# Weights of the shared and the first expert requested piece by piece along the token loop of a fused cross-attention and mixture-of-experts kernel

## Chip, cores and metric

One core of one Trainium2 chip. The metric is the device time of one execution in microseconds (us); lower is better.

## What is computed

The input is `x` (8 batches of 256 tokens, 256 wide, float32, so 16 tiles of 128 tokens) with a context of 77 keys per batch. Two residual layers follow each other, each behind a layer norm:

```python
x = x + tanh(g_xattn) * attention(layernorm(x), ctx, ctx, mask, Wq, Wk, Wv, Wo, ...)   # 16 heads of 16
x = x + tanh(g_ffn)   * ffn(layernorm(x), ...)
# ffn of a token row t:
#   combine = the top 2 of softmax(t @ gate_w.T) over 8 experts, renormalised
#   out  = sum over e of combine[e] * (gelu(t @ W1[e] + b1[e]) @ W2[e] + b2[e])   # 256 -> 1024 -> 256
#   out += gelu(t @ sW1 + sb1) @ sW2 + sb2                                        # the shared expert
```

## The kernel before

The five engines run programs of their own, written out by hand in the source, with counting semaphores between them. Nothing is reordered: the order of the code is the order on each engine and on each engine's DMA queue.

**Setup (to about 52 us).** The context is transposed and keys and values are projected. The keys make a round trip through memory (`move_keys`, lines 299 to 306: `moved_k` out, three pieces of `kstack` back in). The queries of a token tile make such a trip too: `move_queries(t)` (308 to 319) on SyncE (SP) waits until the query tile is written, stores it to `moved_q` (256 KB), waits until that has landed, and reads three pieces of 128 KB back into `qstack` (line 317), which has two buffers.

**Token loop (about 52 to 217 us).** For each of the 16 token tiles TensorE runs `step(t)` (734 to 792). It starts with `scores(t + 1)` (650 to 661): eight matmuls of `qstack` with `kd`, line 657, for which it needs the three `qstack` pieces of that tile and the `kd` of its batch. In the same step stand the transposes of the probabilities (688), the product with the values (702), `queries(t + 3)` (646), and the output projection (719). Two tiles make a batch. The `kd` of a batch, a block-diagonal arrangement of its keys, is made by GpSimd (POOL) in `key_diag(b)` (417 to 424), line 420, into one of two buffers. `key_diag(b)` for b of 2 and more waits for `scores` of tile 2b - 3. VectorE (DVE) and ScalarE (ACT) work beside this: DVE line 1105 takes the maximum of the scores, 1145 and 1147 add the attention output to the residual `xres`, 1150 and 1153 take its statistics, 1178 writes the normalised `x2row`, 1093 the normalised input of a later tile, and 1137 the spread values in the first steps. SP stores `x2row` (287) and moves the queries of the tile five further on (`keep_and_move`, 323 to 325).

**Experts (about 208 us to the end).** 55 tiles of 128 rows go through `up` (610) and `down` (624): 9 early tiles and 7 late ones through the shared expert, 39 routed ones through experts 0 to 7. Each phase p (0 is the shared expert, p is expert p - 1, 9 is the shared expert again) has two slots of weights. float32 weights are held as a high and a low part. The high part comes straight from memory (`load_hi1`, 427; `load_hi2`, 431), the whole weight comes a second time into a staging buffer (`load_w1`, 368; `load_w2`, 371), and POOL subtracts the one from the other (`split_w1`, line 440; `split_w2`, line 448). Each of the four loads is 1024 KB; `b1` is 512 KB and `b2` 128 KB. Before `split` come waits for both loads. `ready_1` and `ready_2` tell TensorE that a phase may start. There is one staging buffer for `w1` and one for `w2`, so a `load_w1` must follow the `split_w1` of the phase before it.

Loads, `key_diag` and the splits of phases 0 and 1 all stand in POOL's program (412 to 504), so their order there is the order on POOL and on its DMA queue. The phases from 2 on are loaded in a loop (521 to 545) which the token loop has long left. The functions that the change touches:

Of the kernel before, what the change touches and what calls it, by code (L numbers as in the profile page):

```python
# [40 lines left out]
def gated_cross_attention_and_moe(  # L41
# [3 lines left out]
    B, SQ, D = x.shape  # L45
    SK = ctx.shape[1]
    H = 16
    DH = D // H
    E, _, F = W1.shape
    NT = B * SQ // P  # L50
    TB = SQ // P
# [47 lines left out]
    with ExitStack() as stack:  # L99
# [3 lines left out]
        def sem(name):  # L103
            return stack.enter_context(nc.semaphore(name))
# [154 lines left out]
        S = {n: sem(n) for n in names}  # L259
# [5 lines left out]
        def met(engine):  # L265


            engine.wait_ge(S["zero_set"], 1)
# [98 lines left out]
        def _(pool):  # L367
            def load_w1(p, src):
                pool.dma_start(stage1[:], src).then_inc(S["stage1_in"], 16)

            def load_w2(p, src):
                pool.dma_start(stage2[:], src).then_inc(S["stage2_in"], 16)

            sW1_v, sW2_v = chunked(sW1), chunked(sW2)
# [34 lines left out]
            pool.dma_start(gate_r, gate_w).then_inc(S["gate_w_in"], 16)  # L409
            pool.dma_start(bo_bc[:], bo.partition_broadcast(P)).then_inc(S["bo_in"], 16)  # L410
            pool.wait_ge(S["consts"], 14)
            pool.wait_ge(S["x_in1"], 16)
            load_w1(0, sW1_v)
            load_w2(0, sW2_v)


            def key_diag(b):
                if b >= 2:
                    pool.wait_ge(S["s_ps"], TB * (b - 1))
                pool.tensor_tensor(  # L420
                    kd[:, b % 2, :, :, :],
                    kstack[:, :, b * SK:(b + 1) * SK].bitcast(F32).unsqueeze(2).to_broadcast([P, PAIRS, 2, SK]),
                    headsel[:].unsqueeze(1).unsqueeze(3).to_broadcast([P, PAIRS, 2, SK]), ALU.mult
                ).then_inc(S["kd_ready"], 1)


            def load_hi1(s, src):
                pool.dma_start(w1h[:, bass.ds(s, 1), :, :].rearrange("p o c f -> p (o c) f"), src
                               ).then_inc(S["w1h_in"], 16)

            def load_hi2(s, src):
                pool.dma_start(w2hl[:, bass.ds(s, 1), :, 0:D].rearrange("p o c f -> p (o c) f"), src
                               ).then_inc(S["w2h_in"], 16)

            def split_w1(p, s):
                pool.wait_ge(S["stage1_in"], 16 * p + 16)
                pool.wait_ge(S["w1h_in"], 16 * p + 16)
                hi = w1h[:, bass.ds(s, 1), :, :].rearrange("p o c f -> p (o c) f")
                lo = w1l[:, bass.ds(s, 1), :, :].rearrange("p o c f -> p (o c) f")
                pool.tensor_tensor(lo, stage1[:], hi.bitcast(F32), ALU.subtract).then_inc(S["split_w1"], 1)  # L440
                met(pool)
                pool.wait_ge(S["split_w1"], p + 1)

            def split_w2(p, s):
                pool.wait_ge(S["stage2_in"], 16 * p + 16)
                pool.wait_ge(S["w2h_in"], 16 * p + 16)
                both = w2hl[:, bass.ds(s, 1), :, :].rearrange("p o c f -> p (o c) f")
                pool.tensor_tensor(both[:, :, D:2 * D], stage2[:], both[:, :, 0:D].bitcast(F32),  # L448
                                   ALU.subtract).then_inc(S["split_w2"], 1)
                met(pool)  # L450
                pool.wait_ge(S["split_w2"], p + 1)

            def load_b1(s, src):
                pool.dma_start(b1bc[:, bass.ds(s, 1), :].rearrange("p o f -> p (o f)"), src).then_inc(S["b1_in"], 16)

            def load_b2(s, src):
                pool.dma_start(b2bc[:, bass.ds(s, 1), :].rearrange("p o f -> p (o f)"), src).then_inc(S["b2_in"], 16)

            def ready_1(p):
                met(pool)  # L460
                pool.wait_ge(S["b1_in"], 16 * p + 16)
                pool.sem_inc(S["w1_ready"], 1)

            def ready_2(p):
                pool.wait_ge(S["b2_in"], 16 * p + 16)
                pool.sem_inc(S["w2_ready"], 1)
# [9 lines left out]
            pool.wait_ge(S["sel_set"], 2)  # L476
            pool.wait_ge(S["k_stacked"], 48)
            key_diag(0)
            load_b1(0, shared_b[0])
            load_b2(0, shared_b[1])  # L480
            load_hi1(0, sW1_v)
            load_hi2(0, sW2_v)
            key_diag(1)
            split_w1(0, 0)
            load_w1(1, expert_w1(0))
            ready_1(0)
            key_diag(2)
            split_w2(0, 0)
            load_w2(1, expert_w2(0))
            ready_2(0)  # L490
            load_b1(1, expert_b(0)[0])
            load_b2(1, expert_b(0)[1])
            load_hi1(1, expert_w1(0))
            load_hi2(1, expert_w2(0))
            key_diag(3)
            split_w1(1, 1)
            load_w1(2, expert_w1(1))
            ready_1(1)
            key_diag(4)
            split_w2(1, 1)  # L500
            load_w2(2, expert_w2(1))
            ready_2(1)
            for b in range(5, B):
                key_diag(b)

            pool.wait_ge(S["l_sb"], NT)
            pool.iota(tile_i[:], pattern=[[1, TILES], [0, PH - 1]], base=0, channel_multiplier=0).then_inc(S["tiles_set"], 1)
# [902 lines left out]
```

## Time and profile before

| what | value |
|---|---|
| timed runs | 598.23, 609.38, 610.87 us (median 609.38) |
| profiled execution, its own time | 600.51 us |
| its span | 598.9 us |
| TensorE (PE) busy | 538.7 us, 90% of the span |
| DVE busy | 380.0 us, 63% |
| ACT busy | 240.2 us, 40% |
| POOL busy | 224.4 us, 37% |
| moved by DMA | 96.45 MB, mean 161 GB/s |
| PE's share of the chain of waits that ended last | 62% |

The span runs from the first to the last instruction; 1.6 us of the execution lie outside it. TensorE is the engine that most of the time is spent on, and the last two thirds of the span are expert tiles with PE at 98% of the time. The token loop is less full. Times below are us from the start of the span.

### The profile page before, as it was taken

Reading aid. Unit: us, or ns where it says so; the run is one execution under the profiler, and the core shown is the slowest. Engines: PE = TensorE matmul, PEld = TensorE weight load, DVE = VectorE, ACT = ScalarE, POOL = GpSimd, SP = SyncE. Lnnn points to the kernel's source line nnn. Section 1 sums busy time; section 2 is a strip of 40 time slices with the busy share of each in tenths; the row PEclk is TensorE's granted clock in tenths of the full one; section 3 lists DMA queues with packets and bytes.
Section 4 is the critical chain, followed back from the end, with each engine's and each line's share of the span. In section 5 each row is a group of like instructions: output and inputs, shape, how many; then the busy total and the mean of one; then the engine's idle time right before and its main releaser. Section 6 shows DMA issues by size and latency. Waiting matters only on the chain.

```text
span 598.9 us, 12255 instructions
## 1 busy us (share of the span) xinstructions
PE 538.7 (90%) x3223; PEld 467.9 (78%) x3224; DVE 380.0 (63%) x787; ACT 240.2 (40%) x528; POOL 224.4 (37%) x194
## 2 busy tenths in 40 slices
PE   2815968999999869999999999999999999999995
PEld 2615958888888758887888888888888888888884
DVE  7405555888787557766666555655565555655888
ACT  1300234666766443343343434334343434334331
POOL 4106525511100004772534444435444444301773
PEclk9975587989999879999999999999999999999999
DMA  7689295453337332335647674755665665311454
GB/s 239 218 214 254 85 275 149 130 149 105 96 101 241 124 114 72 123 108 164 177 139 237 197 231 125 239 145 172 197 231 156 235 187 195 98 35 51 138 171 122
DMA packets 74358, 96.45 MB, mean 161 GB/s; under 512 B 6125, under 2 KB 61661, under 8 KB 74341
## 3 DMA queue, kind: packets, MB, share of 16 engines
q0 software_dynamic: 23712, 57.18, 31.3%
q1 hardware_dynamic: 44181, 33.94, 19.0%
q10 hardware_dynamic: 6448, 5.12, 2.6%
q8 instruction: 8, 0.13, 0.1%
q14 instruction: 9, 0.07, 0.0%
HBM read 70.04 MB, written 21.97 MB: 154 GB/s over the span
## 4 chain that ended last, share of the span: by engine, by line
PE 62%; POOL 10%; DVE 10%; issue 8%; ACT 5%; DMA 5%; SPq 0%; POOLq 0%; DVEq 0%; ACTq 0%
PE ps L632 13%; PE ps L619 7%; PE ps L620 7%; PE ps L621 7%; PE ps L633 7%; PE ps L607 6%; POOL gath L551 5%; POOL routed_x L515 5%; PE ps L702 3%; PE ps L673 3%; PE ps L646 2%; DMA moved_q<-xT 2%; PE ps L600 2%; PE ps L688 2%; DVE xT L1099 1%
## 5 line engine op out<-in xcount | busy, mean ns | idle before, releaser
L632 PE MATMUL ps<-w2hl,hTh 128*128 (+1 forms) x440 | 162.4, 408 | 2.9 <-DVE hTl L1163 2.9
L633 PE MATMUL ps<-w2hl,hTl 128*128 (+1 forms) x440 | 123.7, 281 | 0.0
L995 ACT ACTIVATE hid<-hid 128x512 f32<-128x512 f32 x110 | 69.2, 632 | 132.2 <-DVE hid L1169 132.2
L632 PEld LDWEIGHTS ps<-w2hl,hTh 128*128 128x128 f32 x440 | 82.9, 188 | 21.4 <-issue 3.7
L989 ACT ACTIVATE hTh<-ps 128x512 fp32r<-128x512 f32 x110 | 60.0, 597 | 95.1 <-PE ps L607 95.1
L1169 DVE TENSOR_TENSOR hid<-ps,b1bc 128x512 f32<-128x512 f32 x110 | 75.3, 689 | 30.2 <-PE ps L621 25.4
L619 PE MATMUL ps<-w1l,xT 128*128 (+1 forms) x220 | 92.6, 421 | 0.0
L620 PE MATMUL ps<-w1h,xT 128*128 (+1 forms) x220 | 87.6, 398 | 0.0
L621 PE MATMUL ps<-w1h,xT 128*128 (+1 forms) x220 | 87.2, 396 | 0.0
L633 PEld LDWEIGHTS ps<-w2hl,hTl 128*128 128x128 f32 x440 | 82.9, 188 | 0.0
L1163 DVE TENSOR_TENSOR hTl<-ps,hTh 128x512 fp32r<-128x512 f32 x110 | 70.8, 685 | 0.0
L448 POOL TENSOR_TENSOR w2hl<-stage,w2hl 128x2048 f32 (+1 forms) x10 | 46.0, 4601 | 51.1 <-DMA w2hl<-in_L_ffn_W 46.3
L440 POOL TENSOR_TENSOR w1l<-stage,w1h 128x2048 f32 (+1 forms) x10 | 45.9, 4588 | 46.6 <-DMA w1h<-in_L_ffn_W 36.7
L607 PE MATMUL ps<-ident,hid 128*128 128x128 f32 x440 | 58.0, 275 | 0.0
L1283 DVE TENSOR_TENSOR ysum<-ps,b2bc 128x256 f32<-128x256 f32 x55 | 23.3, 424 | 48.1 <-PE ps L633 48.0
L420 POOL TENSOR_TENSOR kd<-kstack,headsel 128x1232 fp32r<-128x1232 f32 x8 | 18.1, 2257 | 94.4 <-PE ps L657 66.6
L607 PEld LDWEIGHTS ps<-ident,hid 128*128 128x128 f32 x440 | 51.2, 142 | 2.8 <-ACT hid L995 0.3
L1157 DVE TENSOR_TENSOR xT<-ps,xT 128x256 fp32r<-128x256 f32 x55 | 23.3, 424 | 44.7 <-ACT xT L918 44.6
L621 PEld LDWEIGHTS ps<-w1h,xT 128*128 128x128 f32 x220 | 41.8, 190 | 10.2
L619 PEld LDWEIGHTS ps<-w1l,xT 128*128 128x128 f32 x220 | 41.8, 190 | 8.2 <-issue 0.4
L620 PEld LDWEIGHTS ps<-w1h,xT 128*128 128x128 f32 x220 | 42.0, 191 | 7.5
L551 POOL DMA_INDIRECT gath<-routed_y,slot x32 | 31.0, 968 | 44.2 <-DMA routed_y<-yrow 34.8
(166 smaller groups left out, 797.3 us busy)
## 6 DMA issues: line engine op xcount, KB each, us to landing
stage<-in_L_ffn_W POOLq DMA_DIRECT2D x16, 1024.0 KB, 6.3
w1h<-in_L_ffn_W POOLq DMA_DIRECT2D x8, 1024.0 KB, 6.8
w2hl<-in_L_ffn_W POOLq DMA_DIRECT2D x8, 1024.0 KB, 8.0
qstack<-moved_q SPq DMA_DIRECT2D x48, 128.0 KB, 2.4
xrow<-routed_x SPq DMA_DIRECT2D x39, 128.0 KB, 2.3
routed_y<-yrow ACTq DMA_DIRECT2D x39, 128.0 KB, 1.7
routed_x<-zeros SPq DMA_DIRECT2D x6, 768.0 KB, 3.9
stage<-in_L_ffn_sW POOLq DMA_DIRECT2D x4, 1024.0 KB, 6.3
```

Source lines behind the costliest of these rows:

```text
L448: pool.tensor_tensor(both[:, :, D:2 * D], stage2[:], both[:, :, 0:D].bitcast(F32), ALU.subtract).then_inc(S["split_w2"], 1)
L551: pool.indirect_dma_start(out=gath[:, t, k, :], out_offset=None, in_=routed_y, in_offset=bass.IndirectOffsetOnAxis(ap=slot[:, k, t:t + 1], ...
L607: last = nc.tensor.transpose(p_hT[:, n, c, :], hid[:, n, c * P:(c + 1) * P], ident[:])
L619: mm(p_h[:, n, :], xTh[:, c, :], part(w1l, c), start=c == 0, stop=False)
L620: mm(p_h[:, n, :], xTh[:, c, :], part(w1h, c), start=False, stop=False)
L621: last = mm(p_h[:, n, :], xTl[:, c, :], part(w1h, c), start=False, stop=c == C - 1)
L632: mm(p_y, hTh[:, c, :], part(2 * D), start=c == 0, stop=False)
L633: last = mm(p_y[:, 0:D], hTl[:, c, :], part(D), start=False, stop=c == FC - 1)
L989: act.activation(hTh[:, n * (FC // 2):(n + 1) * (FC // 2), :], p_hT[:, n, :, :], ACT.Copy).then_inc(S["hT_hi"], 1)
L995: act.activation(hid[:, n, :], hid[:, n, :], ACT.Gelu).then_inc(S["h_act"], 1)
L1163: tt(hTl[:, part, :], p_hT[:, n, :, :], hTh[:, part, :].bitcast(F32), ALU.subtract).then_inc(S["hT_lo"], 1)
L1169: tt(hid[:, n, :], p_h[:, n, :], b1bc[:, bass.ds(s, 1), n * (F // 2):(n + 1) * (F // 2)].rearrange("p o f -> p (o f)"), ALU.add).then_inc( ...
```

## The change

The three things that POOL asked for during setup (a wait for the second half of `x`, and both staging loads of the shared expert) are gone from there. They and the other loads of phases 0 and 1 stand between the calls of `key_diag`, one to four loads at each. `key_diag(1)` now follows directly on `key_diag(0)`. The two loads into the high parts of phase 0, and the splits of both phases, come one or two calls later than before. Nothing is computed in another way, and no load is added or taken away.

```diff
             pool.wait_ge(S["consts"], 14)
-            pool.wait_ge(S["x_in1"], 16)
-            load_w1(0, sW1_v)
-            load_w2(0, sW2_v)
...
             key_diag(0)
+            key_diag(1)
+            pool.wait_ge(S["x_in1"], 16)
             load_b1(0, shared_b[0])
             load_b2(0, shared_b[1])
+            load_w1(0, sW1_v)
+            key_diag(2)
             load_hi1(0, sW1_v)
+            load_w2(0, sW2_v)
+            key_diag(3)
             load_hi2(0, sW2_v)
-            key_diag(1)
             split_w1(0, 0)
+            ready_1(0)
+            key_diag(4)
             load_w1(1, expert_w1(0))
-            ready_1(0)
-            key_diag(2)
             split_w2(0, 0)
+            ready_2(0)
+            key_diag(5)
             load_w2(1, expert_w2(0))
-            ready_2(0)
             load_b1(1, expert_b(0)[0])
             load_b2(1, expert_b(0)[1])
             load_hi1(1, expert_w1(0))
+            key_diag(6)
             load_hi2(1, expert_w2(0))
-            key_diag(3)
             split_w1(1, 1)
+            key_diag(7)
             load_w1(2, expert_w1(1))
             ready_1(1)
-            key_diag(4)
             split_w2(1, 1)
             load_w2(2, expert_w2(1))
             ready_2(1)
-            for b in range(5, B):
-                key_diag(b)
```

The first place is POOL behind `key_diag(2)`, early in the token loop. Before, its program reads there (`kd` is `key_diag`; `stage` is a staging buffer; `in_L_ffn_sW` are the shared expert's weights, `in_L_ffn_W` the experts'; the second `kd` below is `key_diag(3)`):

```order
L420 TENSOR_TENSOR kd<-kstack,headsel 128x1232
L448 TENSOR_TENSOR w2hl<-stage,w2hl 128x8x256
L372 DMA stage<-in_L_ffn_W 128x8x256
L454 DMA b1bc<-in_L_ffn_b 128x1024
L457 DMA b2bc<-in_L_ffn_b 128x256
L428 DMA w1h<-in_L_ffn_W 128x2x1024
L432 DMA w2hl<-in_L_ffn_W 128x8x256
L420 TENSOR_TENSOR kd<-kstack,headsel 128x1232
```

After the change POOL's program reads, from `key_diag(2)` to `key_diag(5)` (line numbers behind the removed lines are 3 lower):

```order
L417 TENSOR_TENSOR kd<-kstack,headsel 128x1232
L425 DMA w1h<-in_L_ffn_sW 128x2x1024
L372 DMA stage<-in_L_ffn_sW 128x8x256
L417 TENSOR_TENSOR kd<-kstack,headsel 128x1232
L429 DMA w2hl<-in_L_ffn_sW 128x8x256
L437 TENSOR_TENSOR w1l<-stage,w1h 128x2048
L417 TENSOR_TENSOR kd<-kstack,headsel 128x1232
L369 DMA stage<-in_L_ffn_W 128x2x1024
L445 TENSOR_TENSOR w2hl<-stage,w2hl 128x8x256
L417 TENSOR_TENSOR kd<-kstack,headsel 128x1232
```

Five loads behind `key_diag(2)` have become two, and they stand directly behind it, with no split ahead of them. The second place is POOL from `key_diag(3)` of before on to the end of the loop:

```order
L420 TENSOR_TENSOR kd<-kstack,headsel 128x1232
L440 TENSOR_TENSOR w1l<-stage,w1h 128x2048
L369 DMA stage<-in_L_ffn_W 128x2x1024
L420 TENSOR_TENSOR kd<-kstack,headsel 128x1232
L448 TENSOR_TENSOR w2hl<-stage,w2hl 128x8x256
L372 DMA stage<-in_L_ffn_W 128x8x256
L420 TENSOR_TENSOR kd<-kstack,headsel 128x1232 x3
```

The same end of the loop after the change, from `key_diag(5)` on:

```order
L417 TENSOR_TENSOR kd<-kstack,headsel 128x1232
L372 DMA stage<-in_L_ffn_W 128x8x256
L451 DMA b1bc<-in_L_ffn_b 128x1024
L454 DMA b2bc<-in_L_ffn_b 128x256
L425 DMA w1h<-in_L_ffn_W 128x2x1024
L417 TENSOR_TENSOR kd<-kstack,headsel 128x1232
L429 DMA w2hl<-in_L_ffn_W 128x8x256
L437 TENSOR_TENSOR w1l<-stage,w1h 128x2048
L417 TENSOR_TENSOR kd<-kstack,headsel 128x1232
L369 DMA stage<-in_L_ffn_W 128x2x1024
L445 TENSOR_TENSOR w2hl<-stage,w2hl 128x8x256
L372 DMA stage<-in_L_ffn_W 128x8x256
```

Four loads now stand behind `key_diag(5)`, one behind `key_diag(6)` and two behind `key_diag(7)`; the last three `key_diag` had nothing between them before. TensorE's, DVE's, ACT's and SP's programs are unchanged.

## Rows read from the trace of the kernel before

**Rows 1.** The page: TensorE clock granted, 40 slices of 15 us.

```profile
PEclk9975587989999879999999999999999999999999
```

**Rows 2.** Timeline of PE: start, us, engine, line, instruction, form, count, idle before.

```profile
82.68 1.23 PE L673 MATMUL ps<-x,hid 77*128 77x68 f32 x10
91.02 1.96 PE L657 MATMUL ps<-kd,qstack 97*128 97x154 f32 x8 [7.11 <-issue]
```

**Rows 3.** Timeline of SP's DMA queue: start, us of issuing, line.

```profile
75.00 0.40 SPq L312 DMA_DIRECT2D moved_q<-xT  x1
77.38 1.80 SPq L317 DMA_DIRECT2D qstack<-moved_q  x3
82.05 0.40 SPq L312 DMA_DIRECT2D moved_q<-xT  x1
...
116.76 0.43 SPq L312 DMA_DIRECT2D moved_q<-xT  x1
119.12 1.33 SPq L317 DMA_DIRECT2D qstack<-moved_q  x3
```

**Rows 4.** Line 317, the last of three issued from 77.38 (at 78.2).

```profile
DMA to landing us min/median/max: 12.7/12.7/12.7
```

**Rows 5.** The page's DMA issues: count, KB each, median us to landing.

```profile
qstack<-moved_q SPq DMA_DIRECT2D x48, 128.0 KB, 2.4
...
moved_q<-xT SPq DMA_DIRECT2D x16, 256.0 KB, 2.3
```

**Rows 6.** Timeline of POOL, 68 to 80 us.

```profile
68.60 2.24 POOL L420 TENSOR_TENSOR kd<-kstack,headsel 128x1232 fp32r<-128x1232 f32 x1 [5.70 <-PE ps L657]
...
75.89 0.94 POOL L372 DMA_DIRECT2D stage<-in_L_ffn_W  x1 [0.56 <-POOL w2hl L448]
...
78.62 0.95 POOL L432 DMA_DIRECT2D w2hl<-in_L_ffn_W  x1
```

**Rows 7.** Line 372 at 17.42, the second of two staging loads issued in setup.

```profile
DMA to landing us min/median/max: 7.5/7.5/7.5
```

**Rows 8.** Windows from scores to scores: us, PE, PEld, DVE, ACT, POOL, clock, DMA, GB/s.

```profile
83.91:100.66 16.75, 9.64 (x61) 9.47 (x62) 6.19 (x14) 5.61 (x15) 7.03 (x3) 0.69 0.68 184
...
108.80:117.57 8.77, 7.88 (x63) 7.15 (x63) 7.14 (x15) 5.50 (x15) 6.93 (x3) 1.00 0.31 93
117.57:126.09 8.52, 7.86 (x63) 7.13 (x63) 6.89 (x16) 5.40 (x15) 0.81 (x1) 1.00 0.84 224
126.09:135.16 9.07, 9.00 (x61) 8.51 (x62) 7.38 (x15) 5.71 (x15) 2.24 (x1) 0.81 0.26 79
135.16:143.29 8.13, 7.72 (x63) 7.08 (x63) 6.50 (x16) 5.39 (x15) 0.00 (x0) 1.00 0.32 97
143.29:151.97 8.68, 7.81 (x64) 7.08 (x63) 7.05 (x16) 5.50 (x15) 2.24 (x1) 1.00 0.30 91
```

**Rows 9.** Line 317, the three issued from 119.12.

```profile
DMA to landing us min/median/max: 5.3/5.5/5.7
```

**Rows 10.** Line 312, the one issued at 82.05.

```profile
DMA to landing us min/median/max: 11.4/11.4/11.4
```

**Rows 11.** Timeline of POOL and DVE, one step of the loop, and line 1137.

```profile
85.70 0.64 DVE L1137 TENSOR_TENSOR spread_v<-ps,pairmask 128x340 f32<-128x340 f32 x2
...
110.07 2.26 POOL L420 TENSOR_TENSOR kd<-kstack,headsel 128x1232 fp32r<-128x1232 f32 x1 [8.94 <-PE ps L657]
111.43 1.05 DVE L1178 TENSOR_SCALAR x2row<-xres,mv,nw 128x256 f32 x1 [0.70 <-ACT nw L941]
112.29 4.58 POOL L448 TENSOR_TENSOR w2hl<-stage,w2hl 128x2048 fp32r<-128x2048 f32 x1
...
116.98 0.48 DVE L1147 SCALAR_TENSOR_TENSOR xres<-bo_bc,tgate,xres 128x256 f32 x1
```

**Rows 12.** Timeline of POOL and DVE, 283 to 289 us.

```profile
283.40 4.61 POOL L440 TENSOR_TENSOR w1l<-stage,w1h 128x2048 f32 x1 [5.80 <-DMA w1h<-in_L_ffn_W]
286.26 2.02 DVE L1296 SCALAR_TENSOR_TENSOR xres<-yrow,tgate,xres 128x256 f32<-128x256 f32 x1
```

## The prediction

> **What bounds the kernel now.** The clock line of the page comes first, because it shows where TensorE has been idle [rows 1]. From 225 us on it stays at 9; there the expert tiles follow each other without gaps and the change has no instruction. Ahead of that are low digits: 7, 5, 5 in the slices from 30 to 75 us, and an 8 and a 7 in those from 75 to 105 us. The first hollow is setup with the key round trip. The second is inside the token loop, so PE's own timeline is read there [rows 2]. Its last matmuls before the gap end at 83.91; the scores of tile 3 start at 91.02, behind 7.11 us of idle time. The profile calls the wait "issue", which names nothing. But these scores need two things. The first is `kd` for tiles 2 and 3, which is `key_diag(1)`, long done. The second is `qstack` of tile 3. Its pieces are issued by SP from 77.38 on [rows 3], and the last, issued at 78.2, needs 12.7 us [rows 4], so it lands at 90.9. I take that landing to be what PE waited for. The median of such a piece is 2.4 us [rows 5]. What filled the queues is in POOL's timeline: from 75.89 to 79.6 it issues five loads, 3.6 MB, exactly around SP's issue [rows 6].
>
> The windows from scores to scores give the loop's beat [rows 8]. A step in which POOL makes no `kd` takes 8.13 us (135.16 to 143.29), one with it 8.68 us (143.29 to 151.97). The stalled one takes 16.75 us: 7.11 of stall and 9.64 of work, since PE comes back at the lower of its two clock levels (mean grant 0.69). A second, small disturbance is at 117 to 135 us: 8.52 us where 8.13 is usual, then 9.07 where 8.68 is, 0.78 in all. There POOL's 1 MB load behind the split that began at 112.29 delayed `qstack` of tile 7 to 5.3 to 5.7 us [rows 9].
>
> **Part by part.** PE, DVE, ACT and SP keep their programs, so a shift of the end of the token loop carries over to the end of the run. The sum is made against the profiled execution (600.51 us; span 598.9).
>
> *Setup.* 2 MB less are asked for at 16.7 to 18.3. The second of the two landed at 17.42 + 7.5 = 24.9 [rows 7], and the query round trips come after that. The wait that setup ends with is that for the key round trip, which they don't touch. 0; bounds 0 and a gain of 0.5.
>
> *Behind `key_diag(0)` and `key_diag(1)`.* PE works through the spread at the low clock until 75 us and waits for nothing from POOL. The first split goes, `kd` comes sooner. 0.
>
> *Behind `key_diag(2)`.* `kd` ends at 70.8 [rows 6]. Two loads, 2 MB, follow at once, in place of 3.6 MB from 75.89. By the pair in setup they have landed some 0.7 + 7.5 us on, at 79.1 [rows 7]. SP's store of tile 3 is issued at 75.00 [rows 3] among them. It takes 2.3 us when alone [rows 5]; taken as finished when the pair is, it lands at about 79.5. Then 1.33 us of issue and 2.4 us of landing [rows 3, 5] give `qstack` at 83.2, ahead of 83.91, when PE is ready. The stall of 7.11 us goes, and with it the slow restart, 9.64 - 8.68 = 0.96 us. Next late is DVE: with the stall gone, `key_diag(3)` starts before `x2row` of this step, holds it as at 111.43 (1.05 us), and the spread of line 1137 (0.64 us [rows 11]), which hid in the stall, now stands ahead of the scores' maximum. That takes back 0.6. Gain here: 7.5.
>
> *The splits.* All four now stand in the loop. Take the step from 108.80 as a model [rows 8, 11]: `kd` ends at 112.33, the split follows at once, ends at 116.87, and line 1147, which reads two operands from on-chip memory, starts at 116.98, just behind it. In the new order one DMA issue (0.73 to 0.95 us, [rows 6]) stands between `kd` and the split, so the split ends at S + 8.8 to 9.0 (S is the start of the scores) and 1147 is due at S + 8.18. The row for such a meeting is at 286.26: line 1296, likewise with two operands from there, takes 2.02 us instead of 0.48 and ends 0.27 us behind POOL's split [rows 12]. So 1147 would end at S + 9.1 to 9.3 instead of 8.66: 0.4 to 0.6 us. The statistics, `xn` and PE's next transpose hang on it. Four splits: a loss of 2.0. Bounds: 0, if the splits slip past, and 3.3, four times 0.82 (9.0 - 8.18), if nothing of it is absorbed.
>
> The Trainium skill (SBUF — State Buffer, "Who interferes with whom") says the same as a rule: a VectorE instruction with two SBUF inputs and a GpSimd instruction that reads SBUF exclude each other for the whole instruction, and the one issued first wins. Rows 12 agree with it, 2.02 against 0.48 us; it speaks against this change, and without it the loss of 2.0 would be 0.
>
> *Behind `key_diag(5)`.* 2.6 MB in four loads, issued S + 3.5 to S + 6.3. At the rate of the window from 117.57, 224 GB/s with SP's part in it, up to the 300 or so that 2 MB in 7 us of [rows 7] mean, their data need 9 to 12 us, until about S + 14. SP's store is issued at S + 7.96 (116.76 - 108.80), right among them. `qstack` usually lands at S + 10.32 + 1.33 + 2.4 = S + 14.0 [rows 3, 5] and is needed two steps after S, at S + 8.68 + 8.13 = S + 16.8: a slack of 2.8 us. If the store lands at S + 14.8, shortly behind the loads, `qstack` lands at S + 18.5: a wait of 1.7, and 0.4 for the lower clock behind it, as in the step from 126.09. Loss 2.1. Bounds: 0, and 7.3, if the store takes 11.4 us as at 82.05 [rows 10] (S + 7.96 + 11.4 + 3.7 = S + 23.1, a wait of 6.3, plus 0.96). I take 2.1 because at 82.05 three more pieces of SP's own stood ahead of the store, which here do not.
>
> *Single loads behind `key_diag(3)`, `(4)`, `(6)`* are in before S + 10.3 and lie in the slack: 0. *Behind `key_diag(7)`* the second load follows a split, as at 117 us, and costs half of what that did: 0.4. The disturbance of before (0.78) goes, since that load moved.
>
> *The far end.* POOL is through at about 165 us, and the shared expert is first used at 208. Nothing waits.
>
> Sum: 7.11 + 0.96 - 0.6 - 2.0 - 2.1 - 0.4 + 0.78 = 3.75 us less. 600.51 - 3.75 = 596.8 us. The median of the runs shown, 609.38, is 8.9 above the profiled execution, and their lowest, 598.23, 2.3 below. By the same difference that median would become 605.6 and the lowest 594.5.
>
> **Rivals.**
>
> *The loop takes all of it in (gain 8.25).* The splits don't hold 1147 and the four loads behind `key_diag(5)` are in early: 7.11 + 0.96 - 0.6 + 0.78, 592.3 us. For it: the loop had room for two 1 MB loads at a cost of 0.78. Against it: rows 12. The Trainium skill (DMA: Bandwidth & Descriptors, "Anatomy of one DMA") gives 2.0 us + bytes / 436e3 for a load, so an estimated 8.3 us for 2.75e6 bytes, which would be over before `qstack` suffers; the trace disagrees, with 12.7 us for a piece of 128 KB in such company [rows 4].
>
> *The stall only moves a little.* The 2 MB behind `key_diag(2)` are 9.5 us under way and not 7.5, and SP's store is served only behind them: 71.6 + 9.5 + 2.3 + 3.7 = 87.1 for `qstack`, a wait of 3.2 and 0.96 of clock. 600.9 us. For it: the store stands in their midst. Against it: it was issued later than they, and half are through by then.
>
> *The stall moves into the loop, and the kernel is slower.* The four loads behind `key_diag(5)` stop SP's store as at 82.05, and the wait at `scores` of tile 9 costs 7.3 in place of 2.1: 596.8 + 5.2 = 602.0 us. It decides from the point where that wait costs over 5.85 us (3.75 + 2.1). For it: four of the five loads of the old burst are together again, and each step behind has the same slack only. Against it: SP has 256 KB in the queue, not 640.
>
> *The stall is what the runs differ by.* The timed runs lie 12.6 us apart, and a transfer behind 3.6 MB is a likely place for that. Then the high ones of before lose up to 12.6 and the time is 597 against 609.4. For it: nothing else in the trace waits for transfers as long. Against it: one profile can't show it.
>
> **How the numbers follow.** Forecast 0.45, all taken in 0.18, stall moves a little 0.10, slower 0.12, runs differ by the stall 0.15. The range goes from 590 (598.23 less 8.25) to 606 (609.38 less 3.75); both levels of the timed runs are in it. 2% (12 us) is about what a measurement of this kernel can tell from no change. Only the last rival makes it faster by more, 0.15, and 0.05 comes from the gain of 8.25 measured against a high median: 0.20. Slower by over 2% needs the third rival twice over, 0.04. Within 2%: 0.76.
>
> **What would show it.** Right: in the changed kernel's PE timeline no idle time ahead of line 657 near 84 us, and that step at about 9.3 us; DVE's line 1147 (one line number higher) at 0.9 to 1.1 us four times; a wait of one to two us ahead of one 657 near 134 us; the chosen experts' part 3 to 4 us earlier at equal length. Wrong: a gap at 84 to 87 us (2 MB is too much as well), a gap of 5 us or more near 134 us (the stall has moved), or line 1147 at 0.48 throughout (the splits cost nothing).

## The result and the profile after

Four timed runs of the changed kernel took 609.98, 611.59, 611.76 and 614.23 us (median 611.67), the four of before 598.23 to 610.87 (median 606.38). The ratio is 1.0128 with a 95% interval from 1.0073 to 1.0184: slower, though by less than 2%, where 596.8 had been forecast, and 5.7 us beyond the top of the range. Measured again (e5), with 12 runs of the changed kernel and 29 of before, the medians are 606.74 and 604.04 and the ratio 1.0027 [0.9993, 1.0061]. Medians are of all runs; ratios leave out runs more than 1.5% above the fastest of their kernel, so the two need not agree. So the change costs about 3 us, which e5 by itself can't tell from nothing, and the first measurement shows more: the two intervals don't overlap. Both need explaining.

The profiled execution took 611.76 us, its span 610.2. Where do the 11.3 us lie? The start of each `scores` (line 658 now, 657 before) in the PE timeline, with the start of the routing's first rank matmul (line 827, 826 before) as the end of the loop, gives a ledger:

```
start of           before    after   difference   new in this stretch
scores 0            56.11    57.03      +0.92       +0.92
scores 2            75.88    80.07      +4.19       +3.27
scores 3            91.02    92.63      +1.61       -2.58
scores 4           100.66   105.00      +4.34       +2.73
scores 8           135.16   139.02      +3.86       -0.48
scores 10          151.97   159.46      +7.49       +3.63
scores 12          168.78   176.51      +7.73       +0.24
scores 14          184.96   196.60     +11.64       +3.91
rank matmul        226.86   238.39     +11.53       -0.11
```

Behind the loop nothing was lost or won (11.5 there, 11.3 over the whole span). In the loop four stretches grew by over 2 us each (those that end at scores 2, 4, 10 and 14) and the one with the old stall shrank by 2.58. First the clock line of the page, which answers to [rows 1] (40 slices, now 15.3 us each):

```profile
PEclk9965557998997987999999999999999999999999
```

The run of low digits has one 5 more. Before, TensorE had its higher level back in the slice that begins at 75 us; here the slice from 76 to 92 us is at 5 too. The windows from scores to scores (columns as in [rows 8]) show what that is worth:

```profile
67.46:80.07 12.61, 12.61 (x62) 12.29 (x61) 5.27 (x11) 3.63 (x7) 3.83 (x3) 0.50 0.56 182
80.07:92.63 12.56, 12.56 (x68) 12.11 (x67) 6.22 (x13) 4.33 (x10) 0.00 (x0) 0.58 0.21 58
92.63:105.00 12.37, 9.22 (x64) 8.91 (x63) 7.81 (x13) 5.40 (x14) 7.67 (x3) 0.72 0.51 129
```

The first took 9.34 us before, at a mean grant of 0.69, with the same program on PE. The second is the one that held the stall. PE is busy for all of its 12.56 us, so the 7.11 us of idle time are gone; but at the low level the work takes 12.56 us where before it took 8.03 (75.88 to 83.91). The longer stretch at the low clock took 3.27 + 4.53 = 7.8 us. The third has 3.15 us without PE work, and here PE's and the other engines' timelines are to be read together:

```profile
96.88 0.66 PE L640 MATMUL ps<-ident,xn 128*128 128x128 f32 x2 [3.15 <-issue]
```

```profile
93.82 2.26 POOL L417 TENSOR_TENSOR kd<-kstack,headsel 128x1232 fp32r<-128x1232 f32 x1 [20.47 <-PE ps L658]
```

```profile
93.85 2.38 DVE L1179 TENSOR_SCALAR x2row<-xres,mv,nw 128x256 f32<-128x256 f32 x1 [0.63 <-ACT nw L942]
96.15 0.63 DVE L1138 TENSOR_TENSOR spread_v<-ps,pairmask 128x340 f32<-128x340 f32 x2
```

DVE's `x2row`, 0.41 us when alone, starts 0.03 us behind `key_diag(3)` on POOL and ends when that does. The spread values (line 1138, formerly 1137 [rows 11]) stand behind it on DVE, and in the first three steps PE waits for them ahead of `norm_in`, by a semaphore of its own. The profile again says only "issue". Then the burst behind `key_diag(5)`, in the windows and in SP's timeline, with the landing of the store at 138.21 below it:

```profile
139.02:149.44 10.42, 8.05 (x64) 7.22 (x63) 7.70 (x19) 6.10 (x19) 0.00 (x0) 0.96 0.78 263
149.44:159.46 10.02, 10.02 (x62) 9.82 (x62) 5.52 (x11) 5.07 (x12) 7.68 (x3) 0.70 0.69 171
...
176.51:186.20 9.69, 7.86 (x63) 7.13 (x63) 7.76 (x20) 5.82 (x18) 0.92 (x2) 0.99 0.90 233
186.20:196.60 10.40, 10.40 (x62) 10.20 (x62) 5.64 (x14) 5.35 (x14) 0.00 (x0) 0.68 0.42 136
```

```profile
138.21 0.42 SPq L312 DMA_DIRECT2D moved_q<-xT  x1
145.67 1.33 SPq L317 DMA_DIRECT2D qstack<-moved_q  x3
```

```profile
DMA to landing us min/median/max: 7.4/7.4/7.4
```

```profile
149.44 1.98 PE L658 MATMUL ps<-kd,qstack 97*128 x8 [1.83 <-DMA qstack<-moved_q]
```

The store of 256 KB took 7.4 us instead of 2.3, `qstack` was issued at 145.67 and PE waited 1.83 us for it. The step behind this wait takes 10.02 us at a mean grant of 0.70: a short wait costs twice. The same pair of steps stands behind `key_diag(7)`, where PE waits 1.02 us ahead of scores 13 and the next step takes 10.40 us at 0.68.

### The profile page after: what moved, and what is told of

The parts are those of the page before. It is cut to its first block, busy times and chain, and to the rows that moved or that the text cites. A ratio compares the mean times of both kernels' runs of the same rounds, so it can differ in the third digit from the quotient of the medians.

```text
span 610.2 us, 12254 instructions
## 1 busy us (share of the span) xinstructions
PE 550.3 (90%) x3223; PEld 479.9 (79%) x3224; DVE 379.9 (62%) x787; ACT 240.7 (39%) x528; POOL 224.3 (37%) x194
## 4 chain that ended last, share of the span: by engine, by line
PE 63%; POOL 10%; DVE 8%; DMA 8%; issue 6%; ACT 4%; SPq 1%; POOLq 0%; DVEq 0%; ACTq 0%
PE ps L633 13%; PE ps L620 7%; PE ps L621 6%; PE ps L622 6%; PE ps L634 6%; PE ps L608 6%; POOL gath L552 5%; POOL routed_x L516 5%; DMA moved_q<-xT 4%; PE ps L703 3%; PE ps L674 3%; PE ps L689 2%; PE ps L647 2%; PE ps L601 2%; PE ps L658 2%
```

## The experiments

Two questions: is the low clock of this run the change's doing, and which of the moved pieces cost what? They ran in three groups, e1 to e4 on one chip, e5 to e8 and then e9 to e12 on another, beside 35, 29 and 23 runs of before; each ratio is to those of its own group. For the loop alone I compare scores 2 to scores 15 in the profiles (before 116.0 us, after 123.5).

**e1, the kernel before again; e5, the kernel after again.** No edit.

> The kernel before, unchanged, with the granted clock of every run. Theory A (the clock's return): the timed runs of before lay 12.6 us apart because TensorE gets its higher clock back near 72 us in some runs and near 91 us in others. Then low times go with a mean clock near 0.948 and high times with one near 0.93, and the difference is about 8 us. Theory B (transfers): the runs differ by how long the stall behind the 3.6 MB burst lasts; then the mean clock hardly follows the time. Time 598 to 611 us under both.

> The kernel after, unchanged, beside many runs of before on the same chip. Theory A (most of the loss seen so far was the clock coming back late, which is chance): the median lies 2 to 4 us above before, with runs down to 603 and mean clocks from 0.925 to 0.94, as e2 had. Theory C (taking the staging loads out of setup sets the late return of the clock each time): all runs stay near 611 us with a mean clock at 0.925 to 0.93, 5 us or more above before.

e1: 605.51 us, 1.0007 [0.9976, 1.0038]. Over 47 runs of before's instructions (e1's 12 and the 35 beside them, 600.52 to 610.12 us) time and mean clock go together with a correlation of -0.83; the 6 runs at a clock below 0.931 have a median of 609.6, the 12 at 0.941 and more 604.2, 5.4 us apart where theory A had said about 8. The correlation doesn't say in which stretch the clock was low: the profiled executions of e1 and of before lie 6.4 us apart, of which 1.7 us are there at scores 3, 3.7 at scores 15, and the rest comes behind the loop's last scores. The profiled execution of e1 had the clock back near 84 us, not 72: scores 2 at 80.24, as in the changed kernel, with before's own instructions.

```profile
67.62:80.24 12.62, 12.62 (x62) 12.30 (x61) 5.27 (x11) 3.64 (x7) 9.99 (x7) 0.50 0.26 73
```

What the late return does to the stall stands in the row of the next `scores`:

```profile
92.70 1.96 PE L657 MATMUL ps<-kd,qstack 97*128 97x154 f32 x8 [2.75 <-issue]
```

The wait is 2.75 us here, where it was 7.11 [rows 2]: scores 2 began 4.36 us later than in the profile of before, scores 3 only 1.68 later. The stall hides most of a late clock. It also follows that the 7.8 us above are no pure loss against before: scores 3 start at 92.70 us in this late execution of before and at 92.63 in that of the changed kernel.

e5: 606.74 us, 1.0027, runs from 601.59 to 612.09 and mean clocks from 0.926 to 0.942. That is what theory A expected; theory C, all near 611, falls. In e5's profile, too, the clock was late (scores 2 at 80.03).

**e2, the staging loads back in setup.**

```diff
             pool.wait_ge(S["consts"], 14)
+            pool.wait_ge(S["x_in1"], 16)
+            load_w1(0, sW1_v)
+            load_w2(0, sW2_v)
...
             key_diag(1)
-            pool.wait_ge(S["x_in1"], 16)
...
-            load_w1(0, sW1_v)
             key_diag(2)
             load_hi1(0, sW1_v)
-            load_w2(0, sW2_v)
```

> The kernel after, with the two staging loads of the shared expert asked for in setup again; all else of the change stays. Theory A: if taking 2 MB out of setup is what shifts the phase in which the clock comes back, the clock rises near 72 us again and the time falls by 8 us to about 603 to 604. If the clock's return does not hang on setup, 611 us as after. Theory B (the loads in the loop cost it): 611 us, within 1 us of after, since no load of the loop but one is moved.

606.08 us, 1.0030 [0.9992, 1.0068], runs from 602.34 to 611.56: as e5. Its profile had the clock back at 72.0 us and still lost in the loop (120.3 us). Taking the loads out of setup brings and costs nothing that these runs can tell.

**What goes with the late return.** In eleven profiles of kernels without extra PE work (before, after, e1, e2, e5 to e11) the 16 key matmuls of setup start at 13.32 us in each and take 5.86 to 7.45 us in all. They begin at 0.72 us each and change to 0.42 us where the clock first rises, at 16.3 us in e10 and at 19.5 in e1; the sooner it rises, the shorter they take together. These are the shortest (e10) and the longest (e1) of PE's timeline rows:

```profile
13.32 5.86 PE L581 MATMUL ps<-spread_v 128*128 128x308 f32 x16 [3.01 <-DVE spread_v L1044]
```

```profile
13.32 7.45 PE L577 MATMUL ps<-spread_v 128*128 128x308 f32 x16 [3.12 <-DVE spread_v L1040]
```

In the six profiles with 6.54 us or less the clock first rose at 16.3 to 17.7 us and was back after the key trip at 70.9 to 72.3; in the five with 7.11 or more it first rose at 18.8 to 19.5 and was back at 83.8 to 84.4, and at 90.5 in that of after. Both sets hold kernels with and without the changed setup (e6, e7 and e10 are changed and early; e1, e9 and e11 unchanged and late). The first load that was moved out of setup stood at 16.70 us in before, and three of the early profiles had their first rise ahead of that. So the moment of return goes with something that varies between executions, with either program, and in these three was settled before any moved load. Why the changed kernel's first profile returned 6 us later still than the other late ones stays open; e5, the same program, had 83.8. The Trainium skill (TensorE: Matmul & The Clock Gate, "Part 1: The HAM clock gate") says that the gate judges activity in a rhythm that doesn't start with the kernel, which makes its transitions vary from run to run. The eleven profiles agree in so far as the first rise varies by 3.2 us over them at one start of the matmuls. The 0.92 us at scores 0 are of this kind too: before's own program has scores 0 at 57.20 us in e1, later than the changed one.

**e3 and e4, TensorE kept at work during the key trip.**

```diff
             values((6, 7))
+            for _ in range(84):
+                mm(ps[:, 0, :], ones[:], zeros[:].bitcast(BF16), start=True, stop=True)
```

> The kernel before, with 84 matmuls of zeros (128x512, bf16, into PSUM bank 0, which is free there) on TensorE while it waits for the key round trip. Theory A: the clock stays at the higher level from 33 us on, the spread and the first scores (52 to 72 us) take half as long, 10 us less: about 589 us for the span, and the runs lie close together. The stall behind the burst stays or gets longer. Theory B: the clock is not what counts; under 3 us less.

> The kernel after with the same 84 matmuls. Theory A: it loses the 8 us of low clock as well as the 10 of the spread, so about 592 us, and 3 to 4 us above the kept-warm before (11.3 less 7.8). Theory B (the loss of 11.3 us is in transfers and holds): it stays about 11 us above the kept-warm before, some 600 us.

e3: 605.43 us, 1.0016 [0.9982, 1.0051]; e4: 602.73 us, 0.9949 [0.9910, 0.9989]. e3 fits theory B's "under 3 us less", but its profile shows why theory A failed: the clock did not stay up. For e4 neither number came. In e3 the clock was at the higher level from 18.2 us and fell at 55.7, in the spread. PE had paused for 1.23 us ahead of the spread (51.41 to 52.64) and was busy from there on:

```profile
52.00:57.00 5.00, 4.36 (x35) 4.37 (x35) 4.05 (x8) 0.52 (x2) 2.11 (x1) 0.87 1.12 348
57.00:60.00 3.00, 3.00 (x16) 2.88 (x16) 2.97 (x7) 0.94 (x1) 2.45 (x1) 0.50 1.65 309
```

The spread is small matmuls (77 rows, 68 columns). Whether they or the pause ahead of them made the clock fall isn't shown: in e4 it fell at 54.3 behind a pause of 0.89 us, in e12 at 60.4, at the end of a pause of 1.85 us. What was won there (scores 2 at 73.4 and 72.3) was paid back at the end of the loop: from scores 15 to the rank matmul both took 38 us, where before took 34.96. That stretch varies as well, from 34.2 to 39.2 us over the profiles, with the low clock in parts of the time from 197 to 237 us. That the kept-warm after beats the kept-warm before is not explained by such a ledger: their loops take 116.9 and 116.8 us. This stays open; 10 runs each at such a scatter don't settle it.

**e6, the spread ahead of x2row on DVE.**

```diff
             def step(t):
                 ok = lambda u: not isinstance(t, int) or 0 <= u < NT
+                for q in {0: (4, 5), 1: (6,), 2: (7,)}.get(t, ()) if isinstance(t, int) else ():
+                    spread_out(q)
                 if ok(t - 2):
                     norm_two(t - 2)
...
-                for q in {0: (4, 5), 1: (6,), 2: (7,)}.get(t, ()) if isinstance(t, int) else ():
-                    spread_out(q)
```

> The kernel after, with one edit on DVE: in the first steps the spread values (spread_out) are written ahead of x2row (norm_two) and not behind it. If the 3.15 us of idle time ahead of norm_in near 94 us come from x2row being held by key_diag(3), with the spread behind it, that wait goes and the step from scores 3 to scores 4 takes about 9 us and not 12.4: 3 to 4 us less than e5. If PE waited there for something else (its instructions, say), the wait stays and the time is that of e5.

The step from scores 3 to 4 fell from 12.37 (12.36 in e5, 12.71 in e2) to 9.50 us:

```profile
75.19:83.12 7.93, 7.90 (x67) 7.53 (x67) 5.82 (x13) 3.79 (x9) 0.00 (x0) 1.00 0.76 247
83.12:92.62 9.50, 9.00 (x64) 8.69 (x62) 7.82 (x15) 5.75 (x15) 7.66 (x3) 0.82 0.68 173
```

The mechanism is shown: the wait was for the spread values behind the held `x2row`. The first row is the step of the old stall at the high clock, 7.93 us for the 15.14 of before. The timed runs don't confirm 3 us: there are four, between 599.31 and 612.51 (median 609.08, 1.0100 [1.0040, 1.0161], above e5), in step with their clocks (0.945 to 0.921).

**e7, the burst behind key_diag(5) divided in time.**

```diff
             load_w2(1, expert_w2(0))
+            pool.wait_ge(S["s_ps"], 9)
             load_b1(1, expert_b(0)[0])
```

> The kernel after, with POOL waiting for scores 8 between load_w2(1) and the three loads behind it, so that the 2.6 MB burst behind key_diag(5) becomes 1 MB and 1.6 MB. If the burst is what stops SP's store, the steps from scores 8 to 9 and 9 to 10 fall from 10.4 and 10.0 us to 8.2 and 8.7, 3.6 us less than e5. If the single loads do the same harm, at least one wait for qstack of over 1 us stays near there.

605.65 us, 1.0023 [0.9987, 1.0060]. The edit did not help, and the wait that the rival named is what came: the steps stay at 10.41 and 9.85 us, with a wait of 2.14:

```profile
140.46 1.98 PE L659 MATMUL ps<-kd,qstack 97*128 x8 [2.14 <-DMA qstack<-moved_q]
```

But it is another wait than in the kernel after. SP's store for tile 9 had landed at 131.55, undisturbed (2.3 us). The three loads, now issued from 131.46 to 133.3, fell on the reads behind it; below are the three in SP's timeline and the landing of the last:

```profile
131.57 1.33 SPq L317 DMA_DIRECT2D qstack<-moved_q  x3
```

```profile
DMA to landing us min/median/max: 7.6/7.6/7.6
```

It landed at 140.2, just ahead of the scores. The next store, at 137.33, took 5.7 us, but its tile was not due before 150.3 and nothing waited for it. So dividing the burst did free the store; the later part then met the next small transfer. Where the loads stand against SP's stores and reads counts, not how many stand together.

**e10, phase 1's biases and load_hi1 asked for during the spread.**

```diff
             load_w1(0, sW1_v)
+            load_hi1(0, sW1_v)
+            pool.wait_ge(S["b1_in"], 16)
+            pool.wait_ge(S["b2_in"], 16)
+            pool.wait_ge(S["w1h_in"], 16)
+            load_b1(1, expert_b(0)[0])
+            load_b2(1, expert_b(0)[1])
+            load_hi1(1, expert_w1(0))
             key_diag(2)
-            load_hi1(0, sW1_v)
...
             load_w2(1, expert_w2(0))
-            load_b1(1, expert_b(0)[0])
-            load_b2(1, expert_b(0)[1])
-            load_hi1(1, expert_w1(0))
```

> The kernel after, with load_hi1(0) and the biases and load_hi1(1) asked for before key_diag(2), between 53 and 66 us, where PE is busy with the spread and few bytes move. Behind key_diag(2) stands load_w2(0) alone, behind key_diag(5) load_w2(1) alone. If the 4 KB rows of hi1(1) and b1(1) are what slows SP's store near 138 us, the steps from scores 8 to 9 and 9 to 10 take 8.2 and 8.7 us (10.4 and 10.0 in after), 3.5 us less; the wait ahead of norm_in near 94 us stays at 3 us and that near scores 14 at 1. If any load there does it, a wait of 1 to 2 us stays ahead of scores 9.

601.66 us, 0.9950 [0.9911, 0.9989], about 0.8% less than e5. The wait ahead of scores 9 is gone, and the hold (3.15 us ahead of `norm_in`, here at 84 us) stays, as expected. The loss behind `key_diag(7)` stays too, but not as the wait of 1 us that was expected: the reads take 6.4 to 7.5 us again, no wait ahead of `scores` is left, and the step before takes 11.39 us at a grant of 0.70:

```profile
82.86:95.43 12.57, 9.42 (x65) 9.11 (x63) 7.81 (x16) 5.77 (x15) 7.65 (x3) 0.73 0.52 131
129.61:137.73 8.12, 7.70 (x63) 7.07 (x63) 6.50 (x16) 5.39 (x15) 0.00 (x0) 1.00 0.34 105
137.73:146.95 9.22, 9.04 (x64) 8.57 (x63) 7.09 (x15) 5.77 (x15) 7.64 (x3) 0.81 0.77 199
163.90:175.29 11.39, 10.79 (x64) 9.90 (x63) 7.19 (x17) 5.57 (x15) 0.94 (x2) 0.70 0.79 198
```

17.3 us for the two steps from scores 8, where after took 20.4 and 16.9 had been expected. One load of 1 MB is still issued at 124.31, 4.5 us ahead of SP's store at 128.79 and under way until 130.76; the store took 2.6 us. So a single load there does little harm. Whether it is the bytes of the three others or the size of their rows that does the harm, e10 doesn't tell.

**e8, only the old burst of the kernel before divided; e9, the same with e6's edit.**

```diff
             load_w2(1, expert_w2(0))
             ready_2(0)
+            key_diag(3)
             load_b1(1, expert_b(0)[0])
             load_b2(1, expert_b(0)[1])
             load_hi1(1, expert_w1(0))
+            key_diag(4)
             load_hi2(1, expert_w2(0))
-            key_diag(3)
             split_w1(1, 1)
+            key_diag(5)
             load_w1(2, expert_w1(1))
             ready_1(1)
-            key_diag(4)
             split_w2(1, 1)
-            load_w2(2, expert_w2(1))
             ready_2(1)
-            for b in range(5, B):
-                key_diag(b)
+            key_diag(6)
+            load_w2(2, expert_w2(1))
+            key_diag(7)
```

> The kernel before, with only the five-load burst of 76 to 80 us divided: load_w2(1) stays behind key_diag(2), the two biases and load_hi1(1) go behind key_diag(3), load_hi2(1) and the split behind key_diag(4), the rest behind key_diag(5) and (6). Setup and all that is ahead of key_diag(2) stays. If the burst's stall is worth what the profile of before shows (7.11 + 0.96 us) and no new wait takes its place, 5 to 8 us less than before. If the wait ahead of norm_in takes its place as in the kernel after, 3.7 us of that come back: 2 to 4 us less.

> The divided burst of e8 with the DVE edit of e6 (spread values ahead of x2row). In e8 the stall left ahead of scores 3 is 2.05 us, which moves PE past x2row, so the hold by key_diag(3) did not meet it (x2row ran at 85.49, key_diag(3) at 88.12). Theory: the edit brings nothing here, within 1 us of e8's ratio of 0.989. Rival: the hold costs something in e8 as well, 2 to 3 us less than e8.

e8: 599.67 us, 0.9891 [0.9853, 0.9928]; e9: 601.60 us, 0.9910 [0.9872, 0.9948], the same within both intervals. The loop takes 112.6 us in e8 and 111.7 in e9. The single load at 76 us leaves 2.05 us of stall ahead of scores 3 instead of 7.11:

```profile
75.97:86.07 10.10, 8.02 (x68) 7.55 (x67) 7.48 (x17) 5.22 (x14) 0.94 (x1) 0.99 0.70 196
86.07:96.41 10.34, 10.34 (x61) 10.14 (x62) 4.88 (x11) 4.31 (x9) 4.07 (x4) 0.68 0.61 167
```

So the purpose of the change is reached by moving the four loads behind the first out of the burst, and phase 2's two loads later with them. In the profile the two steps take 15.14 + 9.64 us before and 10.10 + 10.34 here, 4.3 us less; the timed runs give 4.4 us between the medians of all runs and 6.6 by the ratio. The expectation had 5 to 8 us. e9's clock came back late (scores 2 at 79.68), so it doesn't repeat e8's early stretch; it had no wait ahead of scores 3.

**e11, loads in the gaps only; e12, e11 with the matmuls of e3.** POOL's part from `key_diag(1)` on is put in a new order in e11; setup is that of before and DVE that of e6:

```python
key_diag(0); load_b1(0, ...); load_b2(0, ...); load_hi1(0, ...); load_hi2(0, ...)
key_diag(1)
split_w1(0, 0); ready_1(0); load_w1(1, ...); load_hi1(1, ...)
split_w2(0, 0); ready_2(0); load_b1(1, ...); load_b2(1, ...); load_w2(1, ...)
key_diag(2); key_diag(3); load_hi2(1, ...)
key_diag(4); split_w1(1, 1); ready_1(1)
key_diag(5); load_w1(2, ...)
key_diag(6); split_w2(1, 1); ready_2(1)
key_diag(7); load_w2(2, ...)
```

> Everything learnt in one kernel: staging loads in setup as before; 3.6 MB of phase 1 asked for between 57 and 68 us; then at most one 1 MB load per key_diag, directly behind it, and each split directly behind its key_diag with no load ahead of it; the spread ahead of x2row. If stalls behind bursts and holds are all there is, the loop loses 7.1 + 1.0 + 0.8 us of before's profile: 8 us less than before, ratio 0.985 to 0.988. If the low clock at the spread and at the end of the loop counts for more, the ratio scatters with the mean clock as before and lies at 0.99.

> e11 with the 84 matmuls of zeros of e3 ahead of the spread. In e3 and e4 the clock fell during the spread all the same (near 57 us) and was back near 69 us in both. So scores 2 come at 72 to 73 us and never at 80: 3 us less than e11 when its clock is back near 72, 7 when it is back near 91. On the median 3 to 5 us less than e11. If the time only moves to other stretches of low clock, no difference to e11.

e11: 595.74 us, 0.9844 [0.9799, 0.9888]; e12: 595.99 us, 0.9852 [0.9813, 0.9891]. Both beat the kernel before, and by these ratios the changed one; e11 lands at the lower edge of what was expected. Its loop takes 111.0 us although its profile had the late clock; no wait for `qstack` is left in it. e12's extra matmuls bring nothing, where 3 to 5 us had been expected: its profile had scores 2 at 77.16 in spite of them.

## Why the prediction was wrong

**The low clock as a constant.** The prediction dealt with the part behind `key_diag(0)` and `key_diag(1)` in a sentence, PE "works through the spread at the low clock until 75 us", and put 0 there. The low level ended at 72.3 us in the one profile it had; in the others it ends between 70.9 and 90.5, in e1, with before's own program, at 84.4. That gave 7.8 us to this profile by chance. The runs of before differ with the clock (correlation -0.83 in e1), and the stall is shorter in the slower profile (2.75 against 7.11 us), so the rival "the stall is what the runs differ by" was wrong. The top of the range was the upper runs of before less the forecast gain, and so left no room for a loss. What the stall is worth hangs on the moment of return too. With an early return scores 3 starts at 83.12 us in a changed kernel (e6) against 91.02 in before, 7.9 us sooner; with a late one at 89.36 (e5) against 92.70 (e1), 3.3 sooner. The prediction took the larger gain for every execution. With the return of the result's own profile, at 90.5, the gain at scores 3 was nothing against e1.

**The stall (7.11 + 0.96).** Right for an early clock. `qstack` was ahead of PE, the idle time went; e6 has the step at 7.93 us. e8 confirms that the burst had caused it.

**The 0.6 us behind it.** This is the first step that failed: 3.7 us (12.37 against 8.68). The prediction named the held `x2row` and the spread behind it, but let them stand only ahead of the scores' maximum. PE waits for that spread itself, ahead of `norm_in`, and sat idle for 3.15 us. e6 confirms it by removing 2.9.

**The splits (2.0).** Right in mechanism, half in size: line 1148 took 0.89, 0.63 and 0.89 us beside the splits of the steps from 113.14, 149.44 and 167.73, where 0.48 is usual: 1.0 in all. It reaches TensorE as forecast: ahead of the next `norm_in` PE sits idle for 0.59, 0.33 and 0.57 us, where 0.18 is usual. The first split, from 96.96, met no line 1148. (The splits come two or three calls of `key_diag` later than before, not one or two; three of the four stood in the loop before, too, without such a meeting.)

**Behind `key_diag(5)` (2.1).** Mechanism and place right, size 3.6 (2.29 + 1.34). The wait was 1.83, close to the 1.7 forecast; the low clock behind it was put at 0.4 and was 1.3, and the step that waits lost another 0.5. e10 takes 3.1 of the 3.6 away.

**Behind `key_diag(7)` (0.4).** The largest miss of the transfers: the stretch from scores 12 to 14 lost 3.9, of which 0.4 belong to the split. The second load there is issued at 177.08, `qstack` pieces issued at 177.89 took 6.2 to 7.2 us instead of 2.4, and PE waited 1.02 us ahead of scores 13, with the slow restart after. The prediction had priced it by the disturbance at 117 us, at half. It was more than four times the whole of that. No run changes these two loads alone. But e8, with no load behind `key_diag(7)`, takes 8.12 + 8.05 us for the two steps from scores 12, as before did; e11, with one, 8.12 + 9.22 and no wait; the kernel after, with two, 9.69 + 10.40.

**The sum.** Without the late clock the ledger reads 11.53 - 0.92 - 7.80 = 2.8 us slower. Its terms are 7.11 + 0.96 won at the stall, 3.69 lost to the hold, 0.48 won from scores 4 to 8 (the disturbance gone, less 0.4 for a split), 3.63 lost behind `key_diag(5)`, 0.24 lost from scores 10 to 12, 3.91 lost behind `key_diag(7)`, and 0.11 won behind that. Against the prediction's 3.75 us less, the misses are 3.1 (hold), 1.5 and 3.1 (transfers), less 1.0 (splits) and 0.1 in small terms: 6.6, and 3.75 - 6.6 is -2.8. The medians of e5 and its before differ by 2.7; that the two agree so well is partly luck, since one sum is of two profiles, the other of runs with early and late clocks. Profiles with the clock's return alike give another reading: scores 15 starts 4.1 us later in e2 than in before (both early) and 5.0 later in e5 than in e1 (both late), while the spans differ by 1.8 and 1.9, because the low clock behind the loop fell differently in each. So the loss is some 2 to 5 us and no closer.

The sign was lost to terms that the prediction had listed, each with a row of the mechanism. The hold was priced at the engine where it begins and not at TensorE, where it ends, and the loads behind `key_diag(5)` and `key_diag(7)` were priced too low for the waits and for the low clock that follows them.

## What to carry to other kernels

Dividing a burst helps only where the pieces stand clear of the small transfers, stores and reads, that something waits for (e7 against e10); look for stretches in which the compute engine is busy with work that needs no transfers, and put the bytes there (e11), before spreading them evenly. Price a wait at the bounding engine, follow every semaphore behind a delayed instruction to it, and add the step that follows at the low clock. Read the granted clock of several executions of the same kernel before taking one profile's stretch of low clock as given.

## What had not been expected of the hardware

TensorE held its higher level from 18.2 to 55.7 us in e3 and lost it in the spread's small matmuls, 3.1 us after a pause of 1.23 us. In the changed kernel's profile it worked from 52.91 us on, without a pause of over 0.4 us, and had the lower level until 90.5 all the same. The clock's return after the key trip took place at 70.9 to 72.3 or at 83.8 to 90.5 us, and which of the two could be told already from the 16 matmuls at 13.32 us (6.54 us or less, 7.11 or more; 11 profiles). A store of 256 KB that takes 2.3 us alone took 5.7 us beside 1.6 MB on another queue (e7), 3.9 to 6.7 beside 2 MB (after and e7; in e7 it was issued 3.6 us behind the first load, in after 5.3), and 7.4 to 8.5 beside 2.6 MB (after and e2).
